# The loop over the batches written out: shared and expert FFN with seven-product Strassen-like up projections, one core

## The reference

```python
def ffn(x, wi0, wi1, wo):            # 512 -> 2048 -> 512
    return gelu(x @ wi0) * (x @ wi1) @ wo

share_out  = ffn(x[b], sWi0, sWi1, sWo)
expert_out = ffn(x[b], Wi0[label[b]], Wi1[label[b]], Wo[label[b]])     # one of the experts
gate_in = concatenate([expert_out[0], share_out[0]])                   # token 0 only
w = softmax(relu(gate_in @ g0) @ g1)                                   # two numbers
out[b] = x[b] + expert_out * w[0] + share_out * w[1]
```

## Time and profile before

| what | value |
|---|---|
| median of 3 executions | 2073.61 us (2072.54 to 2074.24) |
| the profiled execution | 2074.91 us, of which the span of its instructions 2072.4 us |
| PE busy | 2022.7 us, 98% of the span, 13834 matmuls |
| DVE busy | 1632.7 us, 79% |
| ACT busy | 1220.7 us, 59% |
| POOL busy | 86.5 us, 4% |
| mean granted clock of TensorE | 0.985 of full speed |
| moved by DMA | 231.33 MB, mean 112 GB/s |

### The profile page before, as it was taken

The page is one execution under the profiler, slowest core; times in us unless marked ns, Lnnn a source line. Parts: engine busy times, 40 slices in busy tenths (PEclk is TensorE's granted clock), DMA queues, the critical chain, the costliest instruction groups (busy, mean ns, idle before and its releaser), DMA issues.

```text
span 2072.4 us, 37072 instructions
## 1 busy us (share of the span) xinstructions
PE 2022.7 (98%) x13834; PEld 1881.9 (91%) x13834; DVE 1632.7 (79%) x1917; ACT 1220.7 (59%) x1665; POOL 86.5 (4%) x62
## 2 busy tenths in 40 slices
PE   7999999999999999999999999999999999999997
PEld 6999999899998999989999899998999989999996
DVE  8778788687886878868788687886878868788775
ACT  6565566555665566655666556565566655566553
POOL 1001000010000100001000010000100001000000
PEclk9999999999999999999999999999999999999998
DMA  5333333433223332334323332343323432333330
GB/s 193 114 101 112 112 101 94 134 112 122 92 94 132 118 117 92 109 126 124 103 92 117 131 121 92 106 134 115 106 92 122 132 115 92 99 116 133 114 101 31
DMA packets 188063, 231.33 MB, mean 112 GB/s; under 512 B 13266, under 2 KB 152530, under 8 KB 185810
## 3 DMA queue, kind: packets, MB, share of 16 engines
q1 hardware_dynamic: 187858, 228.65, 34.5%
HBM read 220.21 MB, written 8.39 MB: 110 GB/s over the span
## 4 chain that ended last, share of the span: by engine, by line
PE 96%; DVE 2%; issue 1%; ACT 0%; POOLq 0%; DMA 0%; POOL 0%; SPq 0%; DVEq 0%; ACTq 0%
PE ps_out L278 34%; PE ps_c L269 27%; PE ps_p L269 18%; PE ps_v L269 18%; DVE al L493 0%; POOLq L60 0%; DMA a_src<-shared 0%; DVE xl L493 0%; DVE a_src L513 0%; DVE gate_prod L583 0%; DVE a_src L517 0%; ACT ah L365 0%; ACT act L400 0%; DVE a_src L508 0%; DVE hid1l L493 0%
## 5 line engine op out<-in xcount | busy, mean ns | idle before, releaser
L493 DVE TENSOR_TENSOR al<-a_src,ah 128x1536 fp32r<-128x1536 f32 (+1 forms) x388 | 531.2, 1394 | 63.9 <-ACT ah L365 60.7
L365 ACT CAST ah<-a_src 128x1536 fp32r<-128x1536 f32 x381 | 451.8, 1186 | 68.5 <-DVE a_src L513 68.5
L269 PE MATMUL ps_c<-xl,ah 128*128 128x256 f32 x1536 | 437.9, 285 | 14.2 <-issue 14.2
L269 PE MATMUL ps_c<-xh,al 128*128 128x256 f32 x1536 | 435.8, 284 | 9.5 <-issue 4.2
L269 PE MATMUL ps_c<-xh,ah 128*128 128x256 f32 x1536 | 437.0, 285 | 0.0
L269 PEld LDWEIGHTS ps_c<-xl,ah 128*128 128x128 f32 x1536 | 296.1, 193 | 25.0 <-issue 15.4
L269 PEld LDWEIGHTS ps_c<-xh,al 128*128 128x128 f32 x1536 | 295.5, 192 | 23.8 <-issue 9.4
L269 PE MATMUL ps_p<-xh,al 128*128 128x256 f32 x1024 | 293.6, 287 | 8.5 <-DVE xl L493 8.5
L269 PEld LDWEIGHTS ps_c<-xh,ah 128*128 128x128 f32 x1536 | 296.3, 193 | 0.0
L269 PE MATMUL ps_p<-xl,ah 128*128 128x256 f32 x1024 | 293.5, 287 | 0.0
L269 PE MATMUL ps_p<-xh,ah 128*128 128x256 f32 x1024 | 293.5, 287 | 0.0
(11 more groups left out here) (75 smaller groups left out, 3609.6 us busy)
## 6 DMA issues: line engine op xcount, KB each, us to landing
a_src<-shared SPq DMA_DIRECT2D x256, 256.0 KB, 4.3
a_src<-experts SPq DMA_DIRECT2D x256, 256.0 KB, 4.1
raw_wo<-shared SPq DMA_DIRECT2D x128, 256.0 KB, 2.9
raw_wo<-experts SPq DMA_DIRECT2D x128, 256.0 KB, 2.7
x_src<-x_cols SPq DMA_DIRECT2D x32, 256.0 KB, 5.4
x_res<-x_rows SPq DMA_DIRECT2D x8, 1024.0 KB, 10.5
out<-s_out SPq DMA_DIRECT2D x7, 1024.0 KB, 8.5
g_sb<-g_rows SPq DMA_DIRECT2D x1, 2048.0 KB, 9.0
```

The costliest lines, as they stand in the source:

```text
L269: mm = nc.tensor.matmul(ps[:, a * HALF:(a + 1) * HALF], a_op[ap][:, i, a, k, :], x_op[xp][:, i, k, :], start=(fresh and a == 0 and k == 0 ...
L365: nc.scalar.copy(a_op[HI][:, i:j, :, :, :], a_src[s][:, i:j, :, :, :]).then_inc(a_hi_done, 1)
L493: nc.vector.tensor_tensor(to, of, hi.bitcast(F32), ALU.subtract).then_inc(done, 1)
```

## The change

`schedule` no longer builds a loop on the engine. It calls `one_pass` 16 times with plain numbers, so that every step of SP, PE, ACT and DVE stands in the program once, and all wait counts and batch indices are constants. The order of the passes and of all work within them is the same.

```diff
-            if isinstance(m, int) and m == 0:
+            if m == 0:
...
-        def schedule(eng, one_pass):
-
-            one_pass(0, SHARED, 0, True, False)
-            with eng.Fori(0, BATCH - 1) as b:
-                one_pass(b, EXPERT, b * (2 * STEPS) + STEPS, False, False)
-                one_pass(b + 1, SHARED, b * (2 * STEPS) + 2 * STEPS, False, False)
-            one_pass(BATCH - 1, EXPERT, N_STEPS - STEPS, False, True)
+        def schedule(one_pass):
+
+            for b in range(BATCH):
+                one_pass(b, SHARED, b * (2 * STEPS), b == 0, False)
+                one_pass(b, EXPERT, b * (2 * STEPS) + STEPS, False, b == BATCH - 1)
...
-            schedule(sp, one_pass)
+            schedule(one_pass)
...
-            schedule(pe, one_pass)
+            schedule(one_pass)
...
-            schedule(sc, one_pass)
+            schedule(one_pass)
...
-                laps = n0 // 2 if isinstance(n0, int) else b * STEPS + (STEPS // 2 if net == EXPERT else 0)
...
-                    step(n0 + c, c, b, net, first, last, laps + (c + 2) // 2)
+                    step(n0 + c, c, b, net, first, last, (n0 + c + 2) // 2)
...
-            schedule(dve, one_pass)
+            schedule(one_pass)
```

## The result

The written-out kernel takes 2035.07 us, the median of 4 runs (2034.56 to 2035.85); the kernel before took 2073.07 us beside it. The ratio is 0.9819, with a 95% interval of 0.9802 to 0.9836. The forecast was 2035.1 us.

A forecast was written before the change was run, and what follows sets the result against it. TensorE, busy in 98% of the span, was taken as the bound. Six jumps back, 38.5 us together, came off the 2073.61 us median, all other terms nothing, giving 2035.1 us; range 2031.5 to 2042 us.

The forecast's parts named there:

- The price of a jump: At each of six loop jumps back on TensorE: idle time plus slower matmuls, 6.4 us a jump.
- The two gaps: TensorE idle before and within P1 at each jump back: 3.63 us at the first, 21.1 us over six.
- The slower matmuls: Matmuls around and behind the gaps run long: 0.25, 1.12, 1.12 and 0.66 us at the first jump.
- the four between the gaps: Four P1 matmuls between a jump's two gaps take 0.73 instead of 0.48 us; 1.5 us over six.
- The sum: Removing all six jumps back gives 38.4 us by parts, 38.5 us by the step ruler.
- What stands in their place: At the old jump places TensorE simply runs on, as at the loop's entry and exit; cost nothing.
- Constants and registers: Wait counts become constants and register work goes; nothing for TensorE, hidden under matmuls already queued.
- Code in sequence: The longer program's instruction fetches keep up; cost nothing, at most 6.4 us for a place where they don't.
- A: First gaps at the second and fourth jumps are DVE's and stay: 2.7 us, 2037.8 us; chance 0.05.
- B: Gaps go but the low clock stays, only 21.1 us back: 2052.5 us; 0.05 with other half gains.
- C: The jump is cheap, the stall lies elsewhere and the gaps stay: 2073 us, no change; chance 0.02.
- D: TensorE runs out of sequential code at packet ends, 6.4 us a place: 2112 us at 12 places; chance 0.02.

The follow-up runs named there:

- the hint: Kernel before with its loop kept on all engines and a hint ahead of each jump back; 2037.45 us, ratio 0.9834.
- the aligned head: Kernel before with its loop kept, TensorE's loop beginning at the start of a fetch block; 2043.24 us, ratio 0.9862.
- The seven loops of one round: Kernel before with its loop split into seven one-round loops on each engine, nothing jumping back; 2035.46 us, ratio 0.9832.
- the empty loops: Written-out kernel plus empty-body loops on TensorE at the six old jump places; 2034.59 us with 2 rounds, 2164.24 us with 60.
- R = 12: Written-out kernel plus an empty loop of 12 rounds on TensorE at each of the six places; 2045.94 us.
- R = 7: Written-out kernel plus an empty loop of 7 rounds on TensorE at each of the six places; 2034.65 us.
- both empty loops at R = 7: Written-out kernel plus, at six places on TensorE, an empty loop of 7 rounds and, after 4 matmuls of P1, one of 8; 2052.68 us.

## Why the prediction was right

**The price of a jump, 6.4 us.** Right, and each of its parts was made or taken away by itself. The two gaps (3.5 us) are two fetches: the hint removes both, the aligned head the second, and beside each lies its packet. The slower matmuls (2.9 us) follow from the standing. They are not all the clock's: the four between the gaps ran at a granted clock of 1.00 and still took 0.25 us too long. That the clock fell while the engine stood is true of before, and not of every place where TensorE alone loops.

**The sum.** The places gave back all of the 38.5 us. The span fell by 39.6 us, 2072.4 to 2032.8. Of the other 1.1 us, 0.7 us are of the start (L426 of step 2 comes at 45.70 us, have 46.42) and 0.3 us of the end (2032.8 - 1996.73 = 36.1 instead of 36.4 us). No run shows a cause in the change; step 2 comes anywhere from 45.4 to 46.9 us in the kernels above. That the forecast of 2035.1 us is met to 0.1 us is luck. The gain was put at 38.5 us and measured at 38.0 us, from a median of before of 2073.07 us and not 2073.61, and by its span the profiled run was forecast 1 us too long.

**What stands in their place.** Nothing, as the entry and exit of the loop had said. The exact case, this change of pass in the middle of the program with a new x to load, stood in before only behind a jump; DVE and ACT were in time for it at all six places.

**Constants and registers** at nothing: right, by the kernel with the hint. The seven loops of one round say nothing about it.

**Code in sequence** at nothing: right; 109 packets and no gap. In "Runtime: NRT & Kernel Launch", section Instruction fetch mechanics, the Trainium skill says that a taken branch out of the loaded blocks waits for a fetch. The hint and the aligned head agree, with 0.00 and 1.3 us a jump instead of 6.4. In "Advanced Engine Details and Errata", section Control Flow Timing, the Trainium skill gives a compare-and-branch about 108 ns. The traces have other values, and they decide: on TensorE about 0.08 us when it isn't taken, 0.21 us back to code a few instructions away, and 3.50 to 4.00 us at the jumps of before.

**The rivals.** A (DVE really late at two places): fallen. The gap is gone, and gaps made on purpose are put down to DVE's low part in the same way, 6 of 6 in two kernels. B (a clock that falls on its own rhythm): fallen, the mean clock is 0.995. C and D fell with the result.

**What I had too simple.** I read each gap as the fetch's length. By the empty loops the sequencer is 2.8 us ahead where the first gap begins, and the gap is 1.15 us in the mean. So the first fetch should hold it for about 4.0 us; the jumps themselves take 3.50 to 4.00 us, 3.73 us in the mean. This didn't enter the sum, since that went by gaps, but it spoiled the expectations with R = 12, with R = 7 and with both empty loops at R = 7.

## What to carry to other kernels

Look for gaps on the bounding engine that come once a round with no awaited event, and count the slower matmuls behind them: here these were 2.9 of 6.4 us. The cheapest evidence that the jump is guilty is in the trace already: where the loop is entered and left, and in how long the branch itself takes. If the program mustn't grow, a hint for the jump back gave over nine tenths of the gain (a ratio of 0.9834 against 0.9819). On an engine with slack the loop may stay, as here on DVE, ACT and SP. And look whether an experiment's program holds what the experiment is about: the count of instructions told here that one didn't.

## What the runs showed of the hardware

- A compare-and-branch on TensorE took 3.50 to 4.00 us to a target whose code wasn't there, 0.34 to 0.39 us with the hint, 0.21 us back over a few instructions, and 0.07 to 0.09 us when it wasn't taken.
- The loss at a jump depends on where the loop's first instruction lies: 1.3 us at the start of a fetch block, and 6.4 us where a second gap came 4 matmuls behind the first.
- A hinted loop pays where it is left, 0.91 us.
- Behind one gap of 0.8 to 1.6 us the granted clock stayed at 1.00, at twelve of twelve places. Behind one of 2.1 to 2.3 us it was low at two of six. Behind 1.2 to 1.3 and 2.2 us with 4 matmuls between them it was low at all six.
- The first matmuls behind a gap took about 0.25 us longer though the granted clock was 1.00.
- TensorE's sequencer ran 2.8 us ahead of its matmuls in these kernels, so up to that much of its own delay was free.
